# Graph layer on Trainium2: ScalarE reads the fourth partial sum ahead of a ReLU and two roundings

## The reference

```
h = relu(layernorm(x))                      # x: 64 x 128 x 1024 float32
x_avg = mean of h over the 64; sim = cosine similarity of its 1024 columns
adj = (sim/2 + 1/2 + gumbel[:, 0]) > (1 - sim/2 - 1/2 + gumbel[:, 1])
common = nmask @ nmask.T                    # nmask = adj or adj.T or identity
W  = adj * where(adj_sym and common > 1, common**2 / max(common), 0)
Wn = dinv[:, None] * W * dinv[None, :]      # dinv = column sums of W ** -1/2
out[b] = Wn.T applied to (h[b].T @ weight) + bias       # weight is the input adj, 128 x 128
return x + out
```

## Time and profile before

| what | value |
|---|---|
| median of 3 runs | 945.06 us (944.86 to 946.09) |
| profiled execution | span 943.7 us; its own device time is not shown apart |
| PE busy | 855.8 us (91%) |
| DVE busy | 775.2 us (82%) |
| ACT busy | 432.5 us (46%) |
| POOL busy | 378.8 us (40%) |
| DMA | 116 GB/s mean |
| granted TensorE clock, mean | 0.970 (of 2.4 GHz) |

### The profile page before, as it was taken

The page is one execution under the profiler, slowest core; times in us unless marked ns, Lnnn a source line. Parts: engine busy times, 40 slices in busy tenths (PEclk is TensorE's granted clock), DMA queues, the critical chain, the costliest instruction groups (busy, mean ns, idle before and its releaser), DMA issues.

```text
span 943.7 us, 13996 instructions
## 1 busy us (share of the span) xinstructions
PE 855.8 (91%) x4808; PEld 443.1 (47%) x4814; DVE 775.2 (82%) x784; ACT 432.5 (46%) x480; POOL 378.8 (40%) x279
## 2 busy tenths in 40 slices
PE   4999977976899999999999999999999999999997
PEld 3445625455445444544444444445444544444453
DVE  7999378699888888888888888888888878888885
ACT  3888522334543444344444444443444444444421
POOL 4888463655433333333333343333333333433330
PEclk9999987975999999999999999999999999999999
DMA  8999510004022222322222222222222422222112
GB/s 350 408 389 374 218 44 1 1 1 178 1 90 90 90 89 89 138 105 98 104 89 89 89 89 89 89 89 89 89 102 100 146 97 89 89 89 90 45 45 90
DMA packets 29108, 109.40 MB, mean 116 GB/s; under 512 B 3360, under 2 KB 3488, under 8 KB 28064
## 3 DMA queue, kind: packets, MB, share of 16 engines
q1 hardware_dynamic: 29088, 109.13, 31.5%
HBM read 75.56 MB, written 33.55 MB: 116 GB/s over the span
## 4 chain that ended last, share of the span: by engine, by line
DVE 33%; issue 28%; POOL 14%; ACT 14%; PE 9%; DVEq 1%; ACTq 1%; POOLq 1%; DMA 0%; SPq 0%
DVE zbuf L935 8%; DVE obuf L947 7%; DVE obuf L977 5%; POOL zbuf L376 5%; ACT ybuf L479 4%; PE ps L702 4%; POOL zbuf L374 4%; ACT hring L464 3%; ACT hring L463 3%; DVE ybuf L943 2%; DVE obuf L981 2%; PE ps L572 2%; POOL ybuf L343 2%; ACT p L493 1%; DVE hring L864 1%
## 5 line engine op out<-in xcount | busy, mean ns | idle before, releaser
L702 PE MATMUL ps<-a,ybuf 128*128 128x512 f16 x2688 | 598.4, 380 | 36.0 <-ACT obuf L493 29.0
L702 PEld LDWEIGHTS ps<-a,ybuf 128*128 128x128 f16 x2688 | 256.2, 98 | 357.4 <-ACT obuf L493 50.4
L479 ACT ACTIVATE ybuf<-zbuf 128x1024 f16<-128x1024 f32 (+1 forms) x128 | 121.6, 950 | 334.1 <-DVE zbuf L935 232.0
L943 DVE TENSOR_TENSOR ybuf<-zbuf,ybuf 128x1024 f16<-128x1024 f32 (+1 forms) x128 | 190.0, 1484 | 60.4 <-ACT ybuf L479 60.4
L374 POOL TENSOR_TENSOR zbuf<-zbuf 128x512 f32<-128x512 f32 x32 | 41.5, 1296 | 453.3 <-DVE zbuf L935 453.3
L864 DVE TENSOR_TENSOR hring<-hring 128x1024 f16<-128x1024 f32 x56 | 72.3, 1291 | 50.2 <-ACT hring L464 50.2
L693 PE MATMUL ps<-w,hring 128*128 128x128 f16 x1344 | 85.5, 221 | 3.6 <-DVE hring L864 3.6
L693 PEld LDWEIGHTS ps<-w,hring 128*128 128x128 f16 x1344 | 79.6, 99 | 18.3 <-DVE zbuf L935 7.7
L493 ACT ACTIVATE obuf<-ps 128x512 f32<-128x512 f32 x96 | 56.3, 586 | 62.6 <-PE ps L702 62.6
L954 DVE SCALAR_TENSOR_TENSOR obuf<-obuf,bias_sb,xring 128x1024 f32<-128x1024 f32 x64 | 82.2, 1285 | 2.9
L377 POOL TENSOR_TENSOR zbuf<-zbuf 128x512 f32<-128x512 f32 x32 | 72.0, 2250 | 0.0
(11 more groups left out here) (144 smaller groups left out, 728.2 us busy)
## 6 DMA issues: line engine op xcount, KB each, us to landing
xring<-in_x_dram SPq DMA_DIRECT2D x96, 512.0 KB, 5.0
out_dram<-obuf SPq DMA_DIRECT2D x64, 512.0 KB, 2.9
ybuf<-in_x_dram SPq DMA_DIRECT2D x28, 512.0 KB, 8.6
a<-in_L_gnn_gumbel_dram SPq DMA_DIRECT2D x8, 1024.0 KB, 14.3
obuf<-in_x_dram SPq DMA_DIRECT2D x4, 512.0 KB, 8.6
w<-in_adj_dram SPq DMA_DIRECT2D x1, 64.0 KB, 1.7
bias_sb<-in_L_gnn_bias_dram SPq DMA_DIRECT2D x1, 0.5 KB, 2.2
```

What stands on the lines that cost most here:

```text
L479: nc.scalar.activation(y16[:, q % 2, 0, a:a + n, :], z[:, a + 1:a + 1 + n, :], ACT.Copy).then_inc(s_yhi, 1)
L702: mm = nc.tensor.matmul(bank[q % 2], y16[:, q % 2, yk, u, c * P:(c + 1) * P], a16[:, ak, mat, c, :], start=(start and c == yk == ak == 0), ...
L943: nc.vector.tensor_tensor(y16[:, q % 2, 1, a:a + n, :], z[:, a + 1:a + 1 + n, :], y16[:, q % 2, 0, a:a + n, :], ALU.subtract).then_inc(s_y, 1)
```

## The change

In `act_pair` the copy `partial(i, q, 3)` stands two steps earlier: behind `y_high(i, q + 1, 1)` and ahead of the second `relu2`, of `y_high(i, q + 1, 2)` and `y_high(i, q + 1, 3)`. No instruction is added or removed.

```diff
@@ act_pair
                 partial(i, q, 2)
                 if ahead1:
                     y_high(i, q + 1, 1)
+                partial(i, q, 3)
                 if ahead2:
                     relu2(i, q + 2, 1)
                 if ahead1:
                     y_high(i, q + 1, 2)
-                partial(i, q, 3)
-                if ahead1:
                     y_high(i, q + 1, 3)
```

## The result

The changed kernel takes **957.08 us** (median of 4 runs, 956.64 to 957.68) against 945.26 us before (4 runs, 944.86 to 946.09): a ratio of 1.0123, 95% interval 1.0108 to 1.0137. It is slower by 11.8 us. The forecast was 956.9 us.

What follows compares the result with a forecast made beforehand. The prediction took the chain of VectorE and ScalarE, not TensorE, to bound the pair. Its terms, 23 x 0.11 + 7 x 1.33 = 11.8 us, added to 945.06, gave 956.9 us, with a range of 950 to 970.

Steps and rivals of the forecast that it cites:

- Product 7's wait is worth nothing: TensorE: 1.32 us idle before product 7 goes in each pair with both ReLUs, booked at nothing; TensorE then waits for `z_of`.
- The copy comes 0.04 behind product 5, and the ReLU 0.79 later: ScalarE, pairs with both ReLUs: copy starts at 628.41, second ReLU at 628.89 instead of 628.10; in q = 2, 3.44 later.
- Price in a pair with both ReLUs: VectorE reaches L947 at 635.81 instead of 635.70: 0.11 us in each of 23 pairs, 2.5 us in all.
- The turns: SBUF port of VectorE and GpSimd: each instruction waits for the other engine's to end; the engine already waiting goes next.
- Price in q = 2: VectorE reaches L947 at 305.04 instead of 303.71: 1.33 us in each of seven pairs, 9.3 us in all.
- The end and the other engines: Last two pairs have no ReLU, TensorE runs 132 matmuls without a gap; DMA and SyncE follow VectorE's outputs: nothing booked.
- the constant part outside the span: Run time beyond the profiled span: median 945.06 us against span 943.7, taken as 1.4 us.
- The sum: Whole kernel: 23 x 0.11 + 7 x 1.33 = 11.8 us, added to 945.06 us.
- The bounds: Pairs with both ReLUs: nothing to 0.79 us each, at most 18.2; q = 2: 1.33 to 3.44, at most 24.1.
- the delay goes through in full: Rival: pairs with both ReLUs pay 0.79 us each, 972.6 us; 987 us if q = 2 does too; chance 0.11.
- GpSimd goes twice: Rival, at the port: L377 then L379 run before `h_low`, 0.29 us per pair with both ReLUs, 961 us; chance 0.10.

## Why the prediction was right

1. *Product 7's wait is worth nothing.* Right. It went, and TensorE waits for `z_of` instead: 1.22 us at 313.66 in the pair shown. The run with less work on TensorE shows the same from the other side.
2. *The copy comes 0.04 behind product 5, and the ReLU 0.79 later.* Measured 0.80, and 3.45 in q = 2 where 3.44 was worked out.
3. *Price in a pair with both ReLUs.* Forecast 0.11, measured 0.10. The turns came as written: L377 undisturbed, `h_low` after it, L379, `y_low`, then L976 alone in 0.68 us.
4. *Price in q = 2.* Forecast 1.33, measured 1.32; 7 pairs, 9.2 us.
5. *The end and the other engines.* Nothing was booked and nothing is left over. Only the first pair of the loop cost 0.25 instead of 0.11. There the copy waits 1.61 us for product 5 instead of 0.21, and `h_low` comes 2.2 us later than before, so that GpSimd did go twice:

```profile
255.28 0.60 ACT L493 ACTIVATE obuf<-ps 128x512 f32<-128x512 f32 x1 [1.61 <-PE ps L701]
...
257.32 1.26 POOL L379 TENSOR_TENSOR zbuf<-zbuf 128x512 f32<-128x512 f32 x1
...
258.24 1.43 DVE L863 TENSOR_TENSOR hring<-hring 128x1024 f16<-128x1024 f32 x1 [2.65 <-ACT hring L464]
```

The 1.4 us that the prediction took as the constant part outside the span compares a span with the time of another execution. For the profiled execution of the changed kernel it is 957.68 - 955.6 = 2.1. The sum added its terms to a median of run times, so nothing hung on it.
6. *The bounds.* The rival "the delay goes through in full" is excluded by the two runs with extra ScalarE copies and by the one in q = 2. "GpSimd goes twice" did not happen in the other 22 of these pairs. The margin was as worked out: `h_low` was ready 0.52 us before L377 ended, and the prediction's times give 631.88 - 631.35 = 0.53. One extra copy, 0.52 us, used it up. So the turn was called rightly, but it hung on half a microsecond, and the price of missing it was the 0.25 us of the first pair. That the total agrees to 0.2 us, about what two medians of the kernel before differ by (945.06 and 945.26), is in part luck.

What the sum did not ask was why the pair was as long as it was. The prediction named the chain through `h_low` and `z_of` rightly, but did not say that VectorE's order in it was open to a change worth 37 us.

## What to carry to other kernels

Before a wait of the busiest engine is removed, ask where that engine waits next; if it is for the chain that sets the period, the wait only moves. Moving an instruction forward in an in-order queue puts its own wait in front of everything that it passes, and the price has to be worked out for each kind of iteration: here the iterations with one step less ahead of the copy paid thirteen times as much. Where two engines take turns at a port, count what both do there; here lateness was nearly free as long as the other one filled it (2.1 us cost 0.26).

## What the runs showed of the hardware

- VectorE's instructions with two SBUF inputs and GpSimd's sums do not run side by side in these traces; the later one waits for the other to end: a 128x1024 subtraction takes 1.23 us alone and up to 2.29 behind a GpSimd instruction, a 128x512 addition 0.68 alone and 1.75 behind one. Where both want to go on, the engine that already waits goes next; in the pair of the changed kernel L379 was issued at 324.30, just before L377 ended, and `h_low`, waiting since 323.81, went ahead of it.
- A turn was lost by 0.05 us (`h_low` at 634.58, GpSimd's next at 634.53), and how late `h_low` was after that did not matter while GpSimd was at work: 22.92 and 22.93 us for lateness that differs by half a microsecond.
- TensorE's granted clock was the full one (1.00, the 2.4 GHz level) in the two pairs of the changed kernel shown, with 1.32 and 1.22 us of idle time before `xw_of`.
